# First layer's bias as two more rows of its product, in a fused decoder block

## What is computed

```
Q = x @ wq + bq ; K = x @ wk + bk ; V = x @ wv + bv        # 16 heads of 16
def prep(t):
    h1 = tanh(einsum('bshd,do->bsho', t, w1) + b1)          # 16 -> 256, same w1 and b1 for every head
    return einsum('bsho,on->bshn', h1, w2) + b2             # 256 -> 16
qp, kp = prep(Q), prep(K)                                   # real and imaginary halves
qe, ke = real parts after a Hadamard product and rotations
qq = sum(qe ** 2, -1) ; kk = sum(ke ** 2, -1)
s = qq[:, :, None, :] * kk[:, None, :, :]
attn = softmax(s / s, axis=2)
x = layernorm(x + (attn @ V) @ wo + bo)
```

## Time and profile before

| what | before |
|---|---|
| median of three runs | 1498.47 us |
| lowest, highest run | 1497.11, 1501.93 us |
| span of the profiled execution | 1494.7 us |
| TensorE matmul busy | 1463.1 us, 98% |
| VectorE busy | 1139.0 us, 76% |
| ScalarE busy | 845.7 us, 57% |
| GpSimd busy | 391.0 us, 26% |
| tanhs of the first phase (L689) | 256, from 18.4 to 327 us |

### The profile page before, as it was taken

How to read it: one execution, slowest core, us unless ns; L and a number is a source line. 1 busy time by engine, 2 the same in 40 slices (tenths; PEclk the granted TensorE clock), 3 DMA queues, 4 the chain that set the end, 5 groups by cost and what they waited for, 6 DMA issues and landing times.

```text
span 1494.7 us, 28692 instructions
## 1 busy us (share of the span) xinstructions
PE 1463.1 (98%) x11013; PEld 1040.2 (70%) x11013; DVE 1139.0 (76%) x2313; ACT 845.7 (57%) x1123; POOL 391.0 (26%) x424
## 2 busy tenths in 40 slices
PE   8999999999999999999999999999999999999998
PEld 5333343435666666666656888898989898898987
DVE  6445544369899999999967888788686878788686
ACT  5888899976888888888873431223222221222221
POOL 1000000124546777666453420000000000000001
PEclk9999999999999999999999999999999999999999
DMA  7765556556656656656652201110010101110001
GB/s 151 149 116 114 106 114 126 94 103 114 108 85 104 109 80 110 107 79 96 98 169 71 78 15 31 28 29 18 22 33 15 40 18 29 28 30 15 21 23 29
DMA packets 89888, 108.62 MB, mean 73 GB/s; under 512 B 18373, under 2 KB 58321, under 8 KB 89753
## 3 DMA queue, kind: packets, MB, share of 16 engines
q1 hardware_dynamic: 89624, 106.61, 37.6%
q10 hardware_dynamic: 128, 0.20, 0.0%
HBM read 26.00 MB, written 4.19 MB: 20 GB/s over the span
## 4 chain that ended last, share of the span: by engine, by line
PE 85%; DVE 7%; ACT 3%; issue 2%; POOL 1%; DMA 1%; SPq 1%; POOLq 0%; DVEq 0%; ACTq 0%
PE ps L109 81%; PE ps L1440 2%; ACT H L689 2%; DVE NM L1670 1%; ACT PX L1612 1%; PE ps L1402 1%; PE ps L1448 1%; SPq L119 1%; DVE EE L856 0%; POOL X L1855 0%; PE ps L1373 0%; DVE GH L2563 0%; DVE GF L2557 0%; DVE GH L2561 0%; DMA ST<-QS 0%
## 5 line engine op out<-in xcount | busy, mean ns | idle before, releaser
L1670 DVE TENSOR_REDUCE NM<-ps 128x4 f32<-128x1024 f32 x256 | 307.3, 1218 | 23.3 <-PE ps L109 22.6
L1612 ACT ACTIVATE PX<-ps 128x1024 f32<-128x1024 f32 x256 | 262.2, 1024 | 72.3 <-PE ps L109 70.5
L689 ACT ACTIVATE H<-ps,b1c 128x1024 f32<-128x1024 f32 x256 | 267.7, 1119 | 39.7 <-PE ps L109 38.2
L2332 ACT ACTIVATE GF<-ps,cols 128x512 f32<-128x512 f32 x128 | 87.2, 687 | 222.1 <-PE ps L109 208.6
L109 PE MATMUL ps<-XC,W_sw_w 128*128 128x512 f32 x768 | 187.1, 393 | 0.0
L109 PEld LDWEIGHTS ps<-XC,W_sw_w 128*128 128x128 f32 x768 | 140.1, 188 | 27.5
L2683 POOL TENSOR_SCALAR RSc<-AGc 128x4 f32<-128x4 f32 x23 | 6.0, 259 | 570.9 <-DVE AGc L2447 570.9
L2327 ACT ACTIVATE GF<-ps 128x512 f32<-128x512 f32 x64 | 38.1, 596 | 185.6 <-PE ps L109 185.6
L2563 DVE TENSOR_TENSOR GH<-GF,GH 128x512 fp32r<-128x512 f32 x192 | 133.9, 697 | 6.6
L109 PE MATMUL ps<-PX,VT 128*32 128x256 f32 x2048 | 137.1, 385 | 0.1
L109 PE MATMUL ps<-KT,QT 48*128 48x512 f32 x512 | 127.6, 496 | 1.9 <-DVE NM L1670 0.9
(11 more groups left out here) (258 smaller groups left out, 2498.1 us busy)
## 6 DMA issues: line engine op xcount, KB each, us to landing
KT<-KS SPq DMA_DIRECT2D x128, 192.0 KB, 4.7
ST<-QS SPq DMA_DIRECT2D x254, 96.0 KB, 2.8
QT<-XSb SPq DMA_DIRECT2D x128, 96.0 KB, 4.2
XR<-TT SPq DMA_DIRECT2D x352, 32.0 KB, 1.9
XT<-in_xT_dram SPq DMA_DIRECT2D x8, 512.0 KB, 4.0
raw_a<-in_x_dram SPq DMA_DIRECT2D x8, 512.0 KB, 4.4
CR<-in_ctxT_dram SPq DMA_DIRECT2D x8, 512.0 KB, 6.0
out_dram<-X SPq DMA_DIRECT2D x7, 512.0 KB, 2.9
```

Of the source, the lines that this page charges most:

```text
L689: e.activation(H1[s % 8][:, :, :], PP[s % 3][:, :, :], ACT.Tanh, bias=b1c[:, half:half + 1], scale=1.0).then_inc(act_th, 1)
L1612: e.activation(PX[s % 3][:, :, :, :], PP[2][:, :, :].rearrange("p g (c q) -> p g c q", c=2), ACT.Exp, bias=0.0, scale=0.25).then_inc(act_e ...
L1670: e.tensor_reduce(NM[u % 2][:, qc, :, :, i], PP[qc][:, :, :].rearrange("p g (m k) -> p g m k", m=2), AX.X, ALU.max, negate=True).then_inc( ...
L2332: e.activation(g[:, :], o, f, bias=cols[:, col:col + 1], scale=1.0).then_inc(act_g, 1)
```

## The change

The bias of the first layer becomes part of the product. The rows 48 and 49 (and 112 and 113) of w1s hold b1, row 49 (113) as its low part by `lomask`; the same rows of the three stack tiles hold ones, written once at the start: GpSimd makes a row of ones in one_a, and SyncE copies it into the stacks by six DMAs (three stacks, two halves), each with 2 rows of 16 times 256 values. The product then reads 50 rows for each c, and the tanh's bias is the number 0.0. The tile b1c, its load, and ScalarE's wait for it go; the counts of two semaphores (d_wts, d_bo) follow, and w1 waits for the six DMAs.

```diff
@@ phase_a
-    b1c = put("b1c", [128, 2])
+    one_a = put("one_a", [2, 256], F32R)
@@ sync
+        def bias_rows(i):
+            w.wait_ge(pool_zero, 2)
+            for c in range(2):
+                dma(e, f32(ST[i][64 * c + 48:64 * c + 50, :, :]).rearrange("r h (x t) -> r (h x) t", t=256),
+                    f32(one_a[:, :]).unsqueeze(1).to_broadcast([2, 16, 256]), d_bo)
...
-        for o, i in ((bqk[:, :, :], a["bqkv"]), (w1r[:, :], a["w1s"]), (b1c[:, :], a["b1c"]), (w2T[:, :, :], a["w2T"]),
+        for o, i in ((bqk[:, :, :], a["bqkv"]), (w1r[:, :], a["w1s"]), (w2T[:, :, :], a["w2T"]),
...
         load_x(1)
+        for i in range(3):
+            bias_rows(i)
         for c, heads in ((0, (0, 1, 2)), (1, (0, 2)), (0, (3, 4, 5)), (1, (4, 5)), (0, (6, 7)), (1, (6, 7))):
             first_stack(e, w, c, heads)
@@ tensor, w1
             w.wait_ge(dve_w1s, 1)
+            w.wait_ge(d_bo, 96)
...
-                t = mm(e, P[2 * b + c][:, :], w1s[64 * c:64 * c + 48, 128 * half:128 * half + 128], ST[n % 3][64 * c:64 * c + 48, q, :], True, True)
+                t = mm(e, P[2 * b + c][:, :], w1s[64 * c:64 * c + 50, 128 * half:128 * half + 128], ST[n % 3][64 * c:64 * c + 50, q, :], True, True)
@@ scalar, step
-            half = s % 4 // 2
-            w.wait_ge(d_wts, 96)
             w.wait_ge(pe_w1, s + 1)
             w.wait_ge(pe_w2, s // 4 - 1)
-            e.activation(H1[s % 8][:, :, :], PP[s % 3][:, :, :], ACT.Tanh, bias=b1c[:, half:half + 1], scale=1.0).then_inc(act_th, 1)
+            e.activation(H1[s % 8][:, :, :], PP[s % 3][:, :, :], ACT.Tanh, bias=0.0, scale=1.0).then_inc(act_th, 1)
@@ gpsimd
         one.done(e.memset(zero[:, :], 0.0), pool_zero)
+        one.done(e.memset(H1[6][0:2, 0, 0:256], 1.0), pool_seq)
+        one.wait()
+        one.done(e.tensor_copy(one_a[:, :], H1[6][0:2, 0, 0:256]), pool_zero)
@@ host arrays
+    lo[[49, 113]] = 1
...
+        w1[64 * k + 48:64 * k + 50] = A["b1"]
```

More of the change, by code:

```diff
@@ L481, in means @@
         def means(m, b, free):
-            w.wait_ge(d_wts, 128)
+            w.wait_ge(d_wts, 112)
             w.wait_ge(dve_xs, 2 * m + 2)
@@ L600, in tensor @@
         free1 = project(0, 1, 7, none)
-        w.wait_ge(d_wts, 96)
+        w.wait_ge(d_wts, 80)
         for h in range(2):
@@ L887, in vector @@
                 w.wait_ge(pe_att, 2 * m)
-                w.wait_ge(d_bo, 64)
+                w.wait_ge(d_bo, 160)
                 e.tensor_tensor(MB[:, :], P[means2_bank(m)][:, 0:256], BO[:, :], ALU.add).then_inc(dve_mb, 1)
@@ L2827, in layout @@
     r["kones"] = ones
-    r["b1c"] = A["b1"].reshape(2, 128).T
     r["bqkv"] = np.stack([A[k].reshape(2, 128).T for k in ("bq", "bk", "bv")], 1)
```

## The result

The changed kernel took 1505.65 us (median of 5 runs, 1504.10 to 1506.69), the kernel before 1498.47 (5 runs, 1497.11 to 1501.99). The ratio is 1.0049, with a 95% interval of 1.0036 to 1.0061: 7.2 us slower, where 0.4 us slower was forecast and 1503.0 was the end of the range. The span of the profiled execution is 1503.8 us, 9.1 over that of before.

The account below looks back on a forecast made before the run. The prediction took TensorE to bound the first phase, with ScalarE second, and stack transfers its start. Span 1494.7 - 2.0 (tanhs) + 2.4 (start) = 1495.1 us, plus 3.8 to the runs' median: 1498.9, range 1494.5 to 1503.0.

Parts of the forecast that it names:

- What bounds the kernel: First phase: TensorE bounds it with ScalarE second, except at its end and its start, where stack transfers count.
- The tanhs: First phase, tanhs without bias pointer: 95 ns less each; 22 after 28 us at 0.09 us give 2.0 us.
- The chain: Chain of work that ended last: it holds 28 of the 256 tanhs, and only a tanh on it gains time.
- Two more rows in the product, the small instructions on GpSimd: w1 reading 50 rows instead of 48, and two small GpSimd instructions hidden by a wait for VectorE: nothing.
- The start: Six ones-row transfers on SyncE ahead of the first stack transfer: 2.4 us cost, bounds 0.3 and 4.9.
- the pile-up: At the start, ones rows pile up on 2 of 16 DMA engines: cost 5.6 us, total 1502.1; chance 0.18.
- the rival's last half sentence: The pile-up with SyncE pushed back too: 1503 us instead of 1502.1.
- My sign for the pile-up: First product after 21 us and stack transfers landing more than 5 us after issue would show the pile-up right.
- The evidence against it: Against the pile-up: an earlier backlog, behind the narrow KT<-ones_b, was a third of this one, its lateness gone soon.
- The other waits: At the start, VectorE's QS waits for stack 0, TensorE's w2 for EE behind it; stack 1 has 0.5 us spare.
- The sum against one span: Whole kernel: profiled span 1494.7 became 1495.1 us, plus 3.8 for the median of the runs: 1498.9.

Follow-up runs that it names:

- e1: Kernel before with the tanh's bias as the number 0.0 and nothing else (first layer's bias left out): 1496.71 us, ratio 0.9981 to before.
- e2: Changed kernel with the tanh's bias pointer and its load back, zeros in the weights' bias rows: 1510.35 us, ratio 1.0064 to before.
- e4_one_row: Changed kernel with one ones row per half and stack instead of two, still six transfers: 1500.57 us, ratio 1.0005 to before.
- e3_rows_early: Changed kernel with the six ones-row transfers moved ahead of the second load of x: 1502.27 us, ratio 1.0021 to before.
- e5: Changed kernel with 40 filler products on TensorE before its first w1 instead of 8: 1503.01 us, ratio 1.0024 to before.
- e8: Changed kernel without any edit, run again as the measure beside others: 1506.36 us, ratio 1.0052 to before.
- e6: Changed kernel with the ones rows written by twelve one-row transfers instead of six of two rows, same place: 1505.15 us, ratio 1.0044 to before.
- e7: Changed kernel with twelve one-row transfers, six on SyncE ahead of the second load of x, six on ScalarE's queue: 1500.62 us, ratio 1.0004 to before.
- e9: e7 with 15 filler products on TensorE instead of 8: 1496.00 us, ratio 0.9987 to before.

## Why the prediction was wrong

*What bounds the kernel.* Right: TensorE with ScalarE beside it, and the stacks' transfers at the start. The change's own cost arose at the start.

*The tanhs: 95 ns less in each, 2.0 us of gain after 28 us.* Right in mechanism, and nearly in size: 92 ns, 2.5 us between the 11th and the last tanh in the changed kernel, 2.7 in all in e1. TensorE still waited 2.6 us for tanhs after 28 us, as I had said (over 2). The chain was the right view: 24 us of busy time went and 2.7 us of time.

*Two more rows in the product, the small instructions on GpSimd.* Nothing, as said: the weight load of 50 rows takes 186 ns, and e1 and e2 leave nothing over for them.

*The start: 2.4 us.* This is the step that failed, by 6 us: at the 11th tanh the changed kernel is 8.4 us late. It has two parts.

The first part is the queue. I priced six issues at 0.65 us each, 3.9 us. That price is right for transfers that nothing holds back: e4_one_row's six took 4.02 us, and its first product was 2.0 us late, inside my 1.4 to 2.9. It also fits the first four of the changed kernel (0.62 to 0.82). The fifth and sixth took 2 us each, since the pile-up, which I had as a rival with a chance of 0.18, was real.

I had its number of DMA engines right. Its rate I had between two rows: 24 GB/s for a DMA engine while x came from HBM, and 12.7 with stacks in flight within SBUF. The 11.5 measured in e3_rows_early lies just under the slower one: 96 KB are then 8.5 us, not 4.1 to 7.7. The length of the runs is not what halves the rate, for runs of 1 KB from HBM moved at 22 GB/s for a DMA engine (the transfers in 6:6.5 of e3_rows_early):

```profile
DMA packets 158, 0.16 MB, mean 324 GB/s; under 512 B 0, under 2 KB 158, under 8 KB 158
...
q1 hardware_dynamic: 158, 0.16, 91.9%
```

And I let the pile-up delay the landing alone, while it held SyncE itself; the rival's last half sentence gave that 0.9 us more without a working. So the first product came at 24.48, over even the rival's 23.2 (from which its 5.6 us late should have been 5.5). My sign for the pile-up was half right for the same reason: the first product came after 21, but SyncE's stack transfers landed 3.6 us after their issue, not more than 5; only the two on ScalarE's queue took 5.6. The evidence against it ("that backlog was a third of this one and the lateness was gone soon") was weak: a third as much work had cost 1.6 us of landing in the earlier trace rows, and it was no reason to take the other end. A larger chance alone would not have been enough, since the rival's own price stopped at 1503.

The second part is the clock, which the prediction didn't have at all: 2 to 3 us (2.6 between e5 and e8 at the 11th tanh). I had reckoned a late first product as late by its own delay, with 0.5 us handed back by the tanhs. After 7.6 us without work TensorE started at half its clock, and did all its work of the next 5 us at that level.

*The other waits (EE behind QS, stack 1 with 0.5 us to spare).* QS did wait for stack 0, 11.02 us instead of 4.13, until 31.61, 6.9 us later than before; it was not what decided: the chain runs through two tanhs (31.04 and 34.94) there.

*The sum against one span.* The span of before, 1494.7, has no late jump in it; with them 1498 is as likely. The median of the runs was the safer base. A run's time is 1.8 us above its own span (1505.65 and 1503.8 for the changed kernel), so 2.0 of the 3.8 us that I added were the chance of a fast execution. That is far less than what the start missed.

## What to carry to other kernels

A transfer that wrote two partitions used two DMA engines here; put into a queue ahead of urgent ones it cost its bytes at 11.5 GB/s for each of them, and the issuing queue's time as well. Splitting it by rows, one partition with 16 runs each, freed the issues but hardly the bytes: they moved at 27 GB/s in all, and an urgent load behind them still waited. What helped was half the bytes and issues (e4_one_row, which leaves out the low part of the bias). When the first use of TensorE is delayed, price the clock too (2.6 us at the 11th tanh here), and keep TensorE fed with filler work until the data is there. And an operation's shortening counts by its appearances in the chain: 256 tanhs lost 24 us, and the kernel 2.7.

## What the runs showed of the hardware

- Two DMA engines moved 23 GB/s together with 1 KB runs from SBUF to SBUF (share 0.12 in 8.5:11.5 of e3), and SyncE's issues then took 1.33 to 1.39 us each, the time of 16 KB at 11.5 GB/s. One-row issues of 16 KB took 0.59 us (e4, e6).
- One-row transfers, 16 runs of 1 KB from one partition to one partition, six on each of two queues, moved 27 GB/s in all at a DMA share of 0.81 (e7, 8:12).
- Runs of 1 KB from HBM moved at 22 GB/s for a DMA engine (324 GB/s at 91.9%, e3, 6:6.5).
- TensorE's granted clock stayed at 1.00 over 0.88 us without work (kernel before, e9) and over 2.83 us (e4), and fell after 1.55 us (0.72 in 18:24, e7; there 1.5 us after the return to work), 3.85 us (e3) and 7.57 us (changed kernel). Back at work, it was at the lower level up to 4.9 us later (e7), 8.5 (e3) and 5.1 us (changed kernel).
- The first w1 group took 1.65 us at the lower level and 0.96 at the full one.
- A tanh of 128x1024 without a pointer took 1027 ns and started 0.90 to 0.92 us after the one ahead of it.
